# Layer 1 attention of a four-layer kernel: VectorE normalises, the cosine products run a slot later as stages of their own, the input split stands ahead of the output rows, and the weight split moves two slots

## What is computed

```
h = _rmsnorm(x, g1) * (1.0 + scale1[:, None, :]) + shift1[:, None, :]
qkv = h @ w_qkv + b_qkv
q, k, v = jnp.split(qkv, 3, axis=-1)
q = _rope(q...); k = _rope(k...)        # o0 = x0*cos - x1*sin, o1 = x1*cos + x0*sin
attn = softmax(q k^T / sqrt(16)); out = attn v
x = x + out @ w_ao + b_ao
```

## Time and profile before

| what | value |
|---|---|
| time of three runs | 2126.70, 2126.88, 2130.39 us |
| the profiled execution's own time | 2127.41 us |
| its span in the profile | 2125.6 us |
| what lies around the span | 1.8 us |
| TensorE busy | 2000.4 us, 94% of the span |
| VectorE, ScalarE, GpSimd busy | 1282.2, 1018.8, 444.4 us |
| mean granted TensorE clock | 0.99 of full speed |

### The profile page before, as it was taken

One profiled execution on the slowest core, in us unless ns is written; L12 is line 12 of the kernel. 1 busy time (PEld: TensorE's weight loads), 2 busy tenths in 40 slices (PEclk: granted clock), 3 DMA queues, 4 the chain that ended last, 5 costly groups with the idle time before them and its releaser, 6 DMA issues.

```text
span 2125.6 us, 44539 instructions
## 1 busy us (share of the span) xinstructions
PE 2000.4 (94%) x15460; PEld 1638.3 (77%) x15460; DVE 1282.2 (60%) x2473; ACT 1018.8 (48%) x1645; POOL 444.4 (21%) x413
## 2 busy tenths in 40 slices
PE   7999999888899999999999989998999999998998
PEld 6887887677777888877777767776888778787887
DVE  5856564666675656545554445455666777775664
ACT  3434555665653333334444444445444555554444
POOL 3632113353530101011111111112011212210000
PEclk9999999999999999999999999999999999999999
DMA  6000000111110000000000000000000000000000
GB/s 223 21 15 8 7 7 31 41 42 39 42 38 11 21 10 20 10 11 7 2 5 7 6 6 1 5 4 13 5 5 10 11 5 10 10 0 7 23 20 30
DMA packets 23543, 42.06 MB, mean 20 GB/s; under 512 B 2322, under 2 KB 13074, under 8 KB 22930
## 3 DMA queue, kind: packets, MB, share of 16 engines
q1 hardware_dynamic: 23442, 40.65, 5.8%
HBM read 28.06 MB, written 4.19 MB: 15 GB/s over the span
## 4 chain that ended last, share of the span: by engine, by line
PE 77%; DVE 10%; issue 6%; ACT 4%; POOL 1%; DMA 0%; DVEq 0%; ACTq 0%; SPq 0%; POOLq 0%
PE psum L607 20%; PE psum L609 19%; PE psum L608 19%; PE psum L702 3%; PE psum L649 3%; PE psum L715 3%; PE psum L734 2%; PE psum L800 2%; PE psum L748 2%; DVE xn L1119 1%; PE psum L691 1%; DVE h_lo L1140 1%; PE psum L542 1%; DVE pb L1189 1%; DVE mx L1186 1%
## 5 line engine op out<-in xcount | busy, mean ns | idle before, releaser
L607 PE MATMUL psum<-h_hi,w_lo 128*128 128x512 f32 x1056 | 435.0, 412 | 19.8 <-DVE h_lo L1140 14.0
L609 PE MATMUL psum<-h_hi,w_hi 128*128 128x512 f32 x1056 | 415.6, 394 | 0.0
L608 PE MATMUL psum<-h_lo,w_hi 128*128 128x512 f32 x1056 | 414.9, 393 | 0.0
L1241 DVE TENSOR_TENSOR hid_lo<-hid,hid_hi 128x512 fp32r<-128x512 f32 x256 | 193.6, 757 | 263.6 <-ACT hid_hi L993 263.6
L993 ACT ACTIVATE hid_hi<-hid 128x512 fp32r<-128x512 f32 x256 | 161.8, 632 | 220.3 <-PE psum L609 131.1
L607 PEld LDWEIGHTS psum<-h_hi,w_lo 128*128 128x128 f32 x1056 | 200.2, 190 | 68.0 <-issue 19.7
L1323 POOL TENSOR_TENSOR rstd<-ms,half_t 128x4 f32<-128x4 f32 x64 | 65.3, 1020 | 892.4 <-DVE ms L1114 484.1
L609 PEld LDWEIGHTS psum<-h_hi,w_hi 128*128 128x128 f32 x1056 | 199.9, 189 | 44.1
L608 PEld LDWEIGHTS psum<-h_lo,w_hi 128*128 128x128 f32 x1056 | 200.6, 190 | 35.0
L1186 DVE TENSOR_REDUCE mx<-psum 128x8 f32<-128x512 f32 x192 | 132.1, 688 | 145.2 <-PE psum L691 116.3
L988 ACT ACTIVATE hid<-psum,vec 128x512 f32<-128x512 f32 x192 | 131.9, 687 | 177.9 <-PE psum L609 164.8
(11 more groups left out here) (144 smaller groups left out, 3649.2 us busy)
## 6 DMA issues: line engine op xcount, KB each, us to landing
swapped<-rows SPq DMA_DIRECT2D x64, 128.0 KB, 2.0
stage<-in_w_dram SPq DMA_DIRECT2D x24, 256.0 KB, 2.7
stage<-in_w_dram SPq DMA_DIRECT2D x8, 512.0 KB, 3.6
out_dram<-xres SPq DMA_DIRECT2D x8, 512.0 KB, 2.9
xres<-in_x_dram SPq DMA_DIRECT2D x1, 3584.0 KB, 18.6
modw_mod<-in_modw_dram SPq DMA_DIRECT2D x2, 1536.0 KB, 13.7
stage<-in_w_dram SPq DMA_DIRECT2D x8, 384.0 KB, 3.3
stage<-in_w_dram SPq DMA_DIRECT2D x8, 192.0 KB, 2.4
```

The costliest lines, as they stand in the source:

```text
L607: nc.tensor.matmul(dst, s_lo, m_hi, start=start and j == 0, stop=False)
L608: nc.tensor.matmul(dst, s_hi, m_lo, start=False, stop=False)
L609: ins = nc.tensor.matmul(dst, s_hi, m_hi, start=False, stop=stop and j == len(pairs) - 1)
L1241: nc.vector.tensor_tensor(hid_lo[:, slot, :], hid32[:, slot, :], hid_hi[:, slot, :].bitcast(F32), ALU.subtract).then_inc(sem["hid"], 1)
```

## The change

ScalarE's `norm` of this phase goes away and VectorE's applies to all phases. The cosine product, until now VectorE's part of `q` and `k`, becomes the stages `q_cos` and `k_cos`, which stand one slot later than `q` and `k`. `k_out 0` and `q_out 0` go behind `k 1` and `q 1` in their slots, and `q_rot 1` behind `stats`. `split` goes from behind pv 1 in slot 4 to ahead of `proj`. `share` and `load` go from the end of slot 2 to the end of slot 4. TensorE's own order stays as it is, and so do the instructions and their number.

```
-        return [own("scores", 0), prev("probs_t", 7), prev("pv", 6), own("k_out", 1), own("q_rot", 1), nxt("stats"),
+        return [own("scores", 0), prev("probs_t", 7), prev("pv", 6), own("q_cos", 1), own("k_out", 1), nxt("stats"),
+                own("q_rot", 1),
                 own("scores", 1), own("probs_t", 0), own("v", 0), prev("pv", 7), own("v_out", 0), own("v", 1), own("v_out", 1),
-                nxt("norm"), own("share"), nxt("load"),
-                own("scores", 2), own("probs_t", 1), prev("merge"), own("q_out", 1), nxt("turn"), own("pv", 0),
-                own("scores", 3), own("probs_t", 2), prev("proj"), own("pv", 1), nxt("split"),
+                nxt("norm"),
+                own("scores", 2), own("probs_t", 1), prev("merge"), nxt("turn"), own("q_out", 1), own("pv", 0),
+                own("scores", 3), own("probs_t", 2), nxt("split"), prev("proj"), own("pv", 1), own("share"), nxt("load"),
                 own("scores", 4), own("probs_t", 3), nxt("k", 0), nxt("k_swap", 0), prev("back"), own("pv", 2),
-                own("scores", 5), own("probs_t", 4), nxt("k_rot", 0), nxt("q", 0), nxt("q_swap", 0), own("pv", 3),
-                own("scores", 6), own("probs_t", 5), nxt("k_out", 0), nxt("q_rot", 0), nxt("k", 1), nxt("k_swap", 1), own("pv", 4),
-                own("scores", 7), own("probs_t", 6), nxt("q_out", 0), nxt("k_rot", 1), nxt("q", 1), nxt("q_swap", 1),
-                own("pv", 5)]
+                own("scores", 5), own("probs_t", 4), nxt("k_cos", 0), nxt("k_rot", 0), nxt("q", 0), nxt("q_swap", 0),
+                own("pv", 3),
+                own("scores", 6), own("probs_t", 5), nxt("q_cos", 0), nxt("k", 1), nxt("k_swap", 1), nxt("q_rot", 0),
+                nxt("k_out", 0), own("pv", 4),
+                own("scores", 7), own("probs_t", 6), nxt("k_cos", 1), nxt("q", 1), nxt("q_swap", 1), nxt("k_rot", 1),
+                nxt("q_out", 0), own("pv", 5)]
...
-                elif s == "norm" and PHASES[ph] == ("attn", 1):
-                    act.wait_ge(sem["rstd"], n_at("rstd", ph, b, 1))
-                    for t in range(TILES):
-                        ins = nc.scalar.activation(xn[:, t, :], xres[:, b * TILES + t, :], ACT.Copy, scale=rstd[:, t:t + 1])
-                    ins.then_inc(sem["normed"], 1)
...
-                elif s == "norm" and PHASES[ph] != ("attn", 1):
+                elif s == "norm":
...
-                elif s in ("q", "k") and layer == 1:
...
+                elif s in ("q_cos", "k_cos"):
```

More of the change, by code:

```diff
@@ L1141, in stage_of @@
                                                 ALU.subtract).then_inc(sem["h"], 1)
-                elif s in ("q", "k") and layer == 1:
-                    bank, at = a_slot(ph, s, k, b)
-                    dve.wait_ge(sem[f"{s}_rows"], n_at(f"{s}_rows", ph, b, k + 1))
-                    dve.wait_ge(sem[s], n_at(s, ph, b, (2 if s == "q" else 4) * k))
-                    nc.vector.scalar_tensor_tensor(by_seq((q32 if s == "q" else k32)[:, :]), by_seq(acc_a[bank]), col(f"{s}1", k),
-                                                   col("cos", 0, S).unsqueeze(1).to_broadcast([P, SEQ, S]),
-                                                   ALU.add, ALU.mult).then_inc(sem[f"{s}_cos"], 1)
-                    dve.wait_ge(sem[f"{s}_cos"], n_at(f"{s}_cos", ph, b, k + 1))
+                elif s in ("q_cos", "k_cos"):
+                    name = s[0]
+                    bank, at = a_slot(ph, name, k, b)
+                    dve.wait_ge(sem[f"{name}_rows"], n_at(f"{name}_rows", ph, b, k + 1))
+                    dve.wait_ge(sem[name], n_at(name, ph, b, (2 if name == "q" else 4) * k))
+                    nc.vector.scalar_tensor_tensor(by_seq((q32 if name == "q" else k32)[:, :]), by_seq(acc_a[bank]),
+                                                   col(f"{name}1", k), col("cos", 0, S).unsqueeze(1).to_broadcast([P, SEQ, S]),
+                                                   ALU.add, ALU.mult).then_inc(sem[s], 1)
+                    dve.wait_ge(sem[s], n_at(s, ph, b, k + 1))
                     dve.sem_inc(sem[f"a_free{bank}"], 1)
```

## The result

| | before | changed |
|---|---|---|
| time, median of 5 runs (lowest to highest) | 2126.70 us (2123.52 to 2130.39) | **2112.98 us** (2109.61 to 2116.23) |
| ratio to before, 95% interval | | 0.9938 (0.9927 to 0.9950) |
| profiled execution: time, span | 2127.41, 2125.6 us | 2109.61, 2107.8 us |

What follows compares the result with a forecast made beforehand. TensorE, with 77% of the chain, was taken as the bound through four pauses per loop block of layer 1's attention. Six loop blocks at +0.8 us (4.9) plus the end blocks made +6.2, hence 2133 us, range 2118 to 2137.

Steps and rivals of the forecast that it cites:

- ScalarE, slots 7 and 8: Layer 1's loop block: bias copies ahead of `k_out 0` and `q_out 0` make scores 0 start 1.42 us later.
- pv 6: Layer 1's loop block: TensorE's 1.18 us pause there goes, moving to scores 0, net +0.1 us.
- stats: Layer 1's loop block: q 1's cosine product now ahead of the statistics, so `ms` ends 0.8 us later.
- norm: Layer 1's loop block: VectorE's `xn` held up by GpSimd's `q_rot 1` addition, so `turn` comes 0.2 us later.
- the order at the split: Between `turn` and k 0: GpSimd's cast goes ahead of VectorE's `h_lo`, costing 0.6 us a loop block.
- x: The start of VectorE's product for `turn`, put 3.4 us behind `turn`; times up to the split count from it.
- its sign of being wrong: The collision at the split resolving the other way in most blocks; the other sign was `q_out 0` through before 469.
- rival 1: At the split `h_lo` beats the cast: -0.9 to -0.7 us a loop block, 2122.8 us in all; chance 0.27.
- The ends: Layer 1's written-out first and last blocks: +0.4 us for the first, +0.9 for the last.
- rival 3: Neither normalising nor the split collides in layer 1's blocks: -1.8 us a block, 2116 us; chance 0.08.
- rival 2: Normalising isn't blocked, cast first at the split: -0.1 us a block, 2127 us; chance 0.15.

Runs made afterwards that it cites:

- e5: The changed kernel with `k_out 0` and `q_out 0` back ahead of `k 1` and `q 1`; 2112.20 us, ratio 0.9946 to the kernel before.
- e8: The changed kernel with `k_out 0` and `q_out 0` ahead of `k 1` and `q 1`, and `q_rot 1` ahead of `stats`; 2108.44 us, ratio 0.9923.
- p2: The changed kernel with 128 semaphore increments at the start of TensorE's program, shifting its code; 2118.59 us, ratio 0.9973.
- p1: The kernel before with 128 semaphore increments at the start of TensorE's program, shifting its code; 2120.21 us, ratio 0.9982.
- e3: The kernel before with only the weight split moved: `share` and `load` behind pv 1 and `split` in slot 4; 2136.49 us, ratio 1.0046.
- e4: The kernel before with only the changed order of `q_cos`, `k_cos`, `q_rot 1`, `k_out 0`, `q_out 0` and `q_out 1`; 2133.92 us, ratio 1.0041.

## Why the prediction was wrong

**Step by step in a loop block.** *ScalarE, slots 7 and 8:* right. Forecast was 1.42 us more ahead of scores 0 and a pause of 1.7; k 0 to scores 0 went from 13.81 to 15.43 (+1.62) with a pause of 1.88, and e5 took it back. *pv 6:* right; its pause is gone, and it follows scores 0 by 1.49 (forecast 1.4). *stats:* `ms` ends 1.1 later against k 0, forecast 0.8. *norm:* right in kind; `xn` took 2.15 (forecast 2.3 to 2.7) beside `q_rot 1`'s addition, and `turn` came 0.44 later against k 0 (26.41 instead of 25.97, forecast 0.2). e8 shows the cause: without the addition in the way, 1.14.

**The step that failed in layer 1 is the order at the split**, "I take the cast first". I had the two requests at x + 2.85 and x + 2.87; they came at x + 2.84 and x + 2.88. `h_lo` starts 0.03 to 0.05 us ahead of the cast and goes first, in all 36 loop blocks of the six profiled executions of the changed kernel, e5, e8 and p2 (cast 1.33 or 1.34 each time). In three of their first blocks the cast came 0.11 or 0.12 ahead, and won each time. So the nominal order decides, at a lead of 0.04 us. The prediction named this as its sign of being wrong. k 0 stood 8.18 behind `turn` where I had 10.1 and rival 1 had 8.4. Rival 1 gave 34.6 us for a block, and 34.59 it was. The Trainium skill (SBUF, "Who interferes with whom"), by which whichever issues first holds the shared ports, gave this outcome, and the trace agrees at 0.04 us. My argument against it was a copy that started 0.02 ahead of `h_lo` and kept its time; read properly, this row says the same as the rule, since the copy came first. I had measured how far ahead of the addition's end `h_lo` asks, and not which of the two comes first.

**The ends.** I gave first and last block +1.3 together. They cost some 4: `xn` of 4.45 in the last, followed by a stretch at a lower clock, and a lost race in the first. I had no term for a third GpSimd instruction behind the addition, though in the last block no `hm` of the next phase stands between `q_rot 1` and the weight split. With this, rival 1's 2122.8 becomes about 2126: layer 1 gained 0.9 us, the kernel as a whole would measure as unchanged. That is inside my range of 2118 to 2137, so the wrong order in layer 1 is not what took the result out of it.

**The step that put the result outside the range** is a term that I set to nothing without a reason: the sum takes all that lies outside layer 1's attention as unchanged, and no rival had anything there. Of the 17.8 us between the two profiled spans 0.9 are of A, 1.2 of what lies behind B, and 15.6 of B: 13.9 in two rounds with code fetches and 1.5 of clock in the last step. My reading of the page passed over "issue 6%" in the chain, and I never looked at B, since the diff doesn't touch it. Repeated, the same two kernels differ by 4 us; with equal fetches (p1, p2) by 1.6 or less.

**The chances.** My 0.31 for "faster" doesn't come out of its parts: half of rival 1's 0.27 and rival 3's 0.08 make 0.215, and rival 2, at 2127, is no change. The gain that was measured has its size from a cause that none of the chances stood for.

## What to carry to other kernels

Where VectorE and GpSimd get in each other's way and ask within hundredths of a microsecond, take the nominal order (it held here down to 0.03 us), and count each instruction that follows without a gap behind the one that wins. Before crediting a small gain to an edit, cut both traces into phases and look at those that the edit doesn't touch, at "issue" pauses and at code packets above all; a few idle instructions at the program's start show whether the place of the code has a part in it. And measure the parts of a mixed change one by one: in layer 1's stretch two of them alone are worth 15 us here, and the whole of it about 1. Profile more than one execution where the times of one kernel spread over 10 us.

## What the runs showed of the hardware that I had not expected

- A loop can be fetched again in some of its rounds and not in others, and where its code lies has a part in it: 16 or 17, 26, 35 or 53 packets for the same stretch, nine more for each such round. A round with fetches takes 6 to 8.5 us more (0.77 to 0.94 us a packet), of which TensorE stands still for 1.3 to 3.7 us at a time, twice in a round; behind that the clock is at its 1.2 GHz level (0.52), which is why 32 small matmuls take 1.13 instead of 0.69 us. 64 increments made that stretch 14.8 us longer, 128 made it 14.5 shorter. The packets are of 16 KB (0.57 MB over 35). A round has 1626 TensorE instructions by the trace, layer 1's loop, which was never fetched again, 614. The Trainium skill (Runtime: NRT & Kernel Launch, "Instruction fetch mechanics") says that TensorE's instruction store holds 128 KiB, is filled in blocks of 16 KiB (256 instructions), and that a taken branch to what isn't in the current window of two pages forces a fetch. By the page's figures a round is an estimated 6.4 of the store's 8 blocks. The runs agree in kind, but not with a window of two pages: such a loop would fetch in each round, and here the changed kernel ran five rounds in a row without one code packet. Why a round that fetches (70.3 us) stands beside one that doesn't (63.9) isn't explained by it.
- The granted clock can fall to the 1.2 GHz level (0.52) behind a pause of 2.16 us, and stay at 1.00 behind one of 2.17 in the block before, at a price of 1.5 us (e3). In e4 it fell behind 1.88 us too.
- GpSimd instructions in a row keep VectorE waiting over all of them where they follow without a gap (4.43 and 4.45 us for 1.14 us of work), and where 0.18 us lay between two of them it took 2.72.
